# A two-layer RWKV and selective-scan stack on one core: the chains of later chunks of layer 2 planned 2.5 slots earlier, PSUM banks picked by release time, one more place in three rings, neighbouring states side by side

## The reference

```
tok = x_embed_conv.reshape(b, c, h * w).transpose(0, 2, 1)      # 3136 tokens, 192 channels
x1, x2 = layernorm(tok, g1, b1), layernorm(tok, g2, b2)
x, z   = x1 @ W_in_x.T, x2 @ W_in_z.T                           # 384 channels each
# per direction (f, and b on the reversed tokens):
xc  = silu(conv_b + causal 4-tap conv of x)
dbl = xc @ W_xproj.T                                            # 12 ranks, 16 B, 16 C
dt  = softplus(dbl[:12] @ W_dt.T + dt_bias)
h_t = exp(dt_t * A) * h_{t-1} + (dt_t * xc_t) * B_t             # 384 x 16 states
y_t = sum_n h_t * C_t + xc_t * D
out = ((y_f + y_b) * silu(z)) @ W_out.T + b_out
```

## Time and profile before

| | |
|---|---|
| median of 3 runs | 20772.64 us (20760.73 to 20794.24) |
| profiled execution | 20745.35 us, of it the span 20743.6 us |
| DVE busy | 17255.4 us, 83% |
| POOL busy | 16916.4 us, 82% |
| PE busy | 16102.5 us, 78% |
| ACT busy | 13201.7 us, 64% |

### The profile page before, as it was taken

One profiled execution on the slowest core, in us unless ns is written; L12 is line 12 of the kernel. 1 busy time (PEld: TensorE's weight loads), 2 busy tenths in 40 slices (PEclk: granted clock), 3 DMA queues, 4 the chain that ended last, 5 costly groups with the idle time before them and its releaser, 6 DMA issues. The chain is left out here.

```text
span 20743.6 us, 188446 instructions
## 1 busy us (share of the span) xinstructions
PE 16102.5 (78%) x45152; PEld 5519.4 (27%) x45152; DVE 17255.4 (83%) x13583; ACT 13201.7 (64%) x33157; POOL 16916.4 (82%) x11028
## 2 busy tenths in 40 slices
PE   7777777777777777777777777777777777777777
PEld 2222222222222222222222222222222222222222
DVE  7888978889787897878878789787887878878788
ACT  5666656666565665656656566565665656666566
POOL 6878968789687896878968789687896978969689
PEclk8888888888888888888888888888888888888888
DMA  2423424234242342423424234242342423424243
GB/s 71 106 61 100 110 61 108 63 96 109 62 108 63 98 107 62 107 63 96 109 62 107 63 97 107 62 107 64 98 106 62 110 63 100 102 62 110 63 102 101
DMA packets 1109659, 1820.18 MB, mean 88 GB/s; under 512 B 189530, under 2 KB 1053556, under 8 KB 1108404
## 3 DMA queue, kind: packets, MB, share of 16 engines
q1 hardware_dynamic: 1108404, 1806.77, 34.7%
HBM read 1083.46 MB, written 245.63 MB: 64 GB/s over the span
## 5 line engine op out<-in xcount | busy, mean ns | idle before, releaser
L1151 DVE TENSOR_TENSOR_SCAN arena<-ps,arena 128x897 f32<-128x897 f32 x5376 | 10982.2, 2065 | 2194.7 <-issue 889.4
L1354 POOL TENSOR_TENSOR arena<-arena 128x896 f32<-128x896 f32 x5376 | 9414.5, 1766 | 428.3 <-DVE arena L1151 386.1
L1285 ACT ACTIVATE ps<-arena,A 128x448 f32<-128x448 f32 x10752 | 6390.3, 627 | 3539.1 <-DVE arena L1151 3426.3
L1057 PE MATMUL ps<-arena,rep 128*64 128x448 f32 x21504 | 5831.6, 673 | 1846.0 <-POOL arena L1354 1842.3
L1346 POOL TENSOR_TENSOR arena<-arena 128x896 f32<-128x896 f32 x2688 | 4761.3, 1772 | 1494.2 <-DMA arena<-arena 1494.2
L1057 PEld LDWEIGHTS ps<-arena,rep 128*64 128x64 f32 x21504 | 1533.7, 160 | 5661.2 <-POOL arena L1354 2884.0
L1140 DVE TENSOR_TENSOR arena<-ps,arena 128x896 f32<-128x896 f32 x2688 | 2864.2, 1066 | 131.3 <-PE ps L977 114.2
L1010 PE MATMUL ps<-arena,diag 128*128 128x448 f32 x5248 | 2308.8, 586 | 270.4 <-DVE arena L1114 227.4
L1010 PEld LDWEIGHTS ps<-arena,diag 128*128 128x128 f32 x5248 | 1040.1, 205 | 1563.1 <-issue 1160.6
L1022 PE MATMUL ps<-arena,wdt 13*128 13x448 f32 x1344 | 848.2, 731 | 641.0 <-DVE arena L1120 561.5
L1049 PE MATMUL ps<-arena,skipd 128*128 128x448 f32 x1344 | 832.5, 707 | 395.2 <-DVE arena L1127 266.6
(11 more groups left out here) (171 smaller groups left out, 18843.0 us busy)
## 6 DMA issues: line engine op xcount, KB each, us to landing
arena<-bc_rows SPq DMA_DIRECT2D x3584, 224.0 KB, 4.2
arena<-arena SPq DMA_DIRECT2D x4160, 112.0 KB, 3.1
x_projected<-arena SPq DMA_DIRECT2D x112, 672.0 KB, 3.5
y_forward<-arena SPq DMA_DIRECT2D x112, 672.0 KB, 3.3
arena<-x_projected SPq DMA_DIRECT2D x112, 672.0 KB, 5.7
arena<-y_forward SPq DMA_DIRECT2D x112, 672.0 KB, 4.3
x<-in_x SPq DMA_DIRECT2D x119, 336.0 KB, 3.7
x_normed<-arena SPq DMA_DIRECT2D x112, 336.0 KB, 2.8
```

The costliest lines, as they stand in the source:

```text
L1057: m = e.matmul(ps[64 * h:64 * h + 64, YBANK, 0:T], rep[:, 0:64], pr[:, (q - 1 + h) % NPR, a * T:a * T + T], start=False, stop=p == NP - 1 ...
L1151: e.tensor_tensor_scan(rev(hh[:, q % NH, 0:W2], s), rev(decays(q)[:, 0:W2], s), rev(bb[:, q % NB, 0:W2], s), car[:, 2 * k + p % 2, n:n + 1 ...
L1285: e.activation(two(decays(q))[:, a, :], dt2[:, r % NR2, p % 2, :], ACT.Exp, scale=Am[s][:, 2 * k + p % 2, n:n + 1]).then_inc(c_ex, 1)
L1354: e.tensor_tensor(pr[:, q % NPR, :].rearrange("p (a b) -> p a b", a=2), two(hh[:, q % NH, :]), cr[:, p - p % 2:p - p % 2 + 2, :], ALU.mult ...
```

## The change

Five things are changed. The planned times of chunks i > 1 start from `PER * (i - 1) - 2.5` instead of `PER * (i - 1)`; the second convolution comes a little later forward and 2.7 slots earlier backward relative to the rest, and gates and output projections are put back by about as much as the chain is moved forward. `dd` is kept from being sent before its place in the ring of three is free. A PE job takes the bank whose last reader is planned to end first, not the other one in turn. `NB`, `NH` and `NPR` become 4, 4 and 6. The two states that lie side by side in a tile become neighbours (states 4k + 2j and 4k + 2j + 1), so that each DMA of `bl` and `cl` reads one run of 896 numbers where it read two of 448; the order of A follows.

```diff
-NB, NH, NPR = 3, 3, 4
+NB, NH, NPR = 4, 4, 6
...
-        sp.extend([(t + 3.4, "dd", i, e), (t + 5, "ud", i, e)])
+        sp.extend([(max(t + 3.4, NP * (EJ * i + e - 2) - 0.5 if i else t), "dd", i, e), (t + 5, "ud", i, e)])
...
-        t = PER * (i - 1) if i else -60
+        t = PER * (i - 1) - 2.5 * (i > 1) if i else -60
...
-            for e, (u, v) in enumerate(((4.2, 6.4), (4.3, 7.4), (6.2, 11))):
+            for e, (u, v) in enumerate(((4.2, 6.4), (4.3, 8.6 if i > 1 else 7.4), (6.2, 11))):
...
-            for e, v in enumerate((1.3, 8.7, 10.7)):
+            for e, v in enumerate((1.3, 6.0, 10.7)):
                 conv(i, e, t + v)
-            project(i, t + 15.6, (1.9, 2.3, 5), 1.5)
+            project(i, t + 15.6, (1.9, 2.3, 5.2), 1.5)
+            t += 2.5
             gate(i, 0, t + 21.6)
-            gate(i, 1, t + 24)
-            gate(i, 2, t + 31)
+            gate(i, 1, t + 26.4)
+            gate(i, 2, t + 33.4)
             for k in range(CJ):
-                o = t + 2 * PER + (4, 6)[k]
+                o = t + 2 * PER + (6.4, 7.9)[k]
...
+    last = dict(n1="nc", n2="nr", x="xe", cv="xc", xp="p1", t="td", z="z4", o="ou")
+    read = {(name, i, e): t for p in plans[1:4] for t, name, i, e in p}
+    release = {(name, i, e): read.get((last.get(name), i, e)) for _, name, i, e in plans[0]}
...
-        b = banks[k % len(banks)]
+        b = banks[k % len(banks)] if t < -10 else min(banks, key=lambda n: until.get(n, -99))
+        until[b] = release[name, i, e]
...
                     e.dma_start(br[64 * j:64 * j + 64, 2 * k:2 * k + 2, :],
-                                cd[i % 2, 4 * k + j:4 * k + 4:2, :].unsqueeze(0).to_broadcast([64, 2, T])).then_inc(s_bl[k], 16)
+                                cd[i % 2, 4 * k + 2 * j:4 * k + 2 * j + 2, :].unsqueeze(0).to_broadcast([64, 2, T])).then_inc(s_bl[k], 16)
```

More of the change, by code:

```diff
@@ L145, in side_schedule @@
     plans = [sorted(p, key=lambda a: a[0]) for p in (pe, act, dve, pool, sp)]
-    jobs, used = {}, {}
+    jobs, used, until = {}, {}, {}
+    last = dict(n1="nc", n2="nr", x="xe", cv="xc", xp="p1", t="td", z="z4", o="ou")
+    read = {(name, i, e): t for p in plans[1:4] for t, name, i, e in p}
+    release = {(name, i, e): read.get((last.get(name), i, e)) for _, name, i, e in plans[0]}
     for k, (t, name, i, e) in enumerate(a for a in plans[0] if a[1] != "dp"):
         banks = WBANK if t >= -10 else [*WBANK, 0, 1, 2, 3]
-        b = banks[k % len(banks)]
+        b = banks[k % len(banks)] if t < -10 else min(banks, key=lambda n: until.get(n, -99))
+        until[b] = release[name, i, e]
         jobs[name, i, e] = (k, b, used.get(b, 0))
@@ L1413, in layer1_sync @@
                     e.dma_start(cr[64 * j:64 * j + 64, 2 * k:2 * k + 2, :],
-                                cd[i % 2, NS + 4 * k + j:NS + 4 * k + 4:2, :].unsqueeze(0).to_broadcast(
+                                cd[i % 2, NS + 4 * k + 2 * j:NS + 4 * k + 2 * j + 2, :].unsqueeze(0).to_broadcast(
                                     [64, 2, T])).then_inc(s_cl[k], 16)
@@ L1523 @@
         arrays[f"alog{s}"] = np.ascontiguousarray(
-            v[l1 + "A_log_" + sfx].reshape(2 * EJ, 64, NP, 2).transpose(3, 1, 0, 2).reshape(128, 2 * EJ, NP))
+            v[l1 + "A_log_" + sfx].reshape(2 * EJ, 64, 4, 2, 2).transpose(3, 1, 0, 2, 4).reshape(128, 2 * EJ, NP))
         arrays[f"vece{s}"] = cols([l1 + "conv_b_" + sfx, l1 + "dt_bias_" + sfx, l1 + "D_" + sfx], 128)
```

## The result

The changed kernel takes 19415.3 us (median of 3 runs, 19388.81 to 19433.57) against 20772.64 before: ratio 0.9344, 95% interval 0.9323 to 0.9365, so 6.6% less. The forecast was 19,760 us and the measured time lies just under the low end of the range, 19,480. The profiled execution took 19415.3 us, its span is 19413.5.

What follows compares the result with a forecast made beforehand. Layer 2 was taken as held up by POOL waiting for `du2` at chunk borders. Gains of 31 + 4.3 + 5.0 + 23 = 63.3 us an image, 1013 us in all, gave 19,760 us, range 19,480 to 20,260.

Steps and rivals of the forecast that it cites:

- The chain: `td`'s end to next chunk's product takes 13.0 us; started 2.5 slots earlier, border wait falls from 5.75 to 0 to 0.4.
- E: Rival: `cl` or the landing, not `td`, binds `ud`, so `du2` arrives as before; 20,770 us within 0.2%, chance 0.04.
- D: Rival: PE stands at a bank so long that `xp` and `t` come late as before; 21,260 us, chance 0.06.
- Border, chunks 1 to 5: The border costs the scans 4.0 us a chunk; with 2.7 for side jobs less 0.5 coupling, 6.2 gained.
- Side jobs of forward chunks: Scan waits at slots 10 to 11 and 18: 1.4 and 1.3 us gained, 2.7 together, bounds 0 and 5.0.
- Chunks 6, 7 and 13: POOL's idle 4.5 and 8.5 us in chunks 6 and 7: 4.3 and 5.0 gained; chunk 13 keeps its time.
- Chunks 8 to 12: POOL's idle 5.8 us a chunk: 4.6 taken, 1.2 left for unevenly placed side jobs; 5 x 4.6 = 23.
- the next link, `ye`, is a slot and more later: 0: Both `o` get one bank, the second waiting about 4 us of PE's time; `ye` comes later, so cost 0.
- Merged rows: `bl` and `cl` landings: bounds 0 and 2.8 us off each, 0.1 by the skill-page estimate; 0 in the sum.
- C: Rival: new waits at banks and `ye` take 3 us a forward, 2 a backward chunk; 20,240 us, chance 0.22.
- B: Rival: POOL is the pace everywhere, ACT stalls nearly go, forward chunks come to 69 us; 19,490 us, chance 0.13.
- A: The main forecast, all terms as summed: 19,760 us, own range 19,560 to 19,980, chance 0.55.

Runs made afterwards that it cites:

- x6: The changed kernel with the chains 1.25 slots earlier instead of 2.5: 20318.42 us, ratio 0.9784 to the kernel before.
- x1: The changed kernel with the old rings (`NB`, `NH`, `NPR` = 3, 3, 4): 19432.49 us, ratio 0.935 to the kernel before.
- x2: The changed kernel with PE's side jobs in banks 6 and 7 in turn, as before: 19638.1 us, ratio 0.9451 to the kernel before.
- x18: The changed kernel with gates and output projections at their old times (24, 31, 4, 6): 19740.68 us, ratio 0.9499 to the kernel before.
- x3: The changed kernel with the old state order, two runs of 448 numbers a `bl` or `cl` DMA: 19432.8 us, ratio 0.9355 to the kernel before.
- x17: The changed kernel with both second convolutions at their old offsets (7.4 forward, 8.7 backward): 19935.91 us, ratio 0.9597 to the kernel before.
- x9: The changed kernel with one more product a chunk (tile 4) on DVE in forward chunks 1 to 6: 19408.47 us, ratio 0.9342 to the kernel before.
- x13: The changed kernel with the third forward convolution at 11.5 instead of 11: 19353.89 us, ratio 0.9314 to the kernel before.

## Why the forecast was too high

The chain was right, and so was the wait at the border itself. The count of 13.0 us from `td` to product against POOL's 14.0 us of work gave a wait of 0 to 0.4 us; measured 0.0 at borders 2 to 13. x6 tests the same count at half the shift and finds it within 0.7 us forward. Product waits (388.7 for 396) follow. Of the other signs, chunks 8 to 12 came as foretold (69.2 us), while the scans' waits through ACT fell not to about 5 us a chunk but to 1.4 (7.1 us in chunks 1 to 5 of image 8). `cl` did not hold SP (E falls), PE was never held long enough to delay `xp` (D falls). The rings at 0 are right (x1).

Per image the traces show 83.1 us gained (spans) where 63.3 were summed. Term by term:

- **Border, chunks 1 to 5.** 4.0 and 1.3 for slot 18, less 0.5, were taken. The two waits gave 4.0 and 1.4 in chunks 2 to 5 and nothing went to coupling; slots 17 to 23 show 4.7, since `nc` has come into them. Right, but not all that a border costs (next term).
- **Side jobs of forward chunks: the step that failed.** The forecast had 8.0 us a chunk of scan waits through ACT before it, treated two of the four places (its slots 10 to 11 and 18, the scans of slots 11 and 19) and put the others at nothing without a reason. Those ahead of the scans of slots 3 and 14 were 1.4 and 1.1 us a chunk, and both went. The first is part of what a border costs, which the forecast had put at 4.0, the scan's own wait at the border, without its echo three slots on. At slot 11 it had 1.4; 3.4 us went and 2.4 came at `xc`, 1.0. Together chunks 2 to 5 gained 10.1 us each where 6.2 were summed: 2.5 by the two waits left out, 0.5 by the coupling that did not come, the rest in smaller waits. Chunk 1, still behind its border wait, gained 5.9. This is the largest error, 3.0 us a chunk in the mean of chunks 1 to 5, 15.1 an image, 242 us in all.
- **Chunks 6, 7 and 13.** 4.3, 5.0 and 0 taken; 5.7, 7.5 and 1.3 measured (image 8 alone, from which the terms were read: 4.2, 9.9 and 1.3). They run at POOL's full load. In chunk 6 the same echo (1.4) went, in chunk 7 also most of the wait at the convolution in its middle, of which the forecast had kept a part: slot 10 goes from 5.8 to 2.5. 5.2 us an image.
- **Chunks 8 to 12.** 4.6 taken, 4.1 measured: a good size, but by luck. Slots 17 to 23 gave 4.4 and slots 0 to 5 1.9, and slots 6 to 9 took 2.0 back. The step "the next link, `ye`, is a slot and more later: 0" failed. x2 shows that the bank choice is worth 2.3 us a chunk there, 184 of its 222 us, because the sum that `ye` reads is not a slot later but behind the third convolution, which stands behind the second `o`. With the banks in turn the gain would have been 1.8. And x18 shows the moved gates, for which the sum had no term, to be worth 322 us. The forecast took a border's gain for granted and counted the edits that keep it as free.
- **Merged rows.** 0 in the sum is right, the bound of 2.8 us off a landing was far off. It came from comparing `bl` with a load of another shape. x3 against after shows 3% of packet time and 0.2 us a landing. The prediction's estimate from the Trainium skill (DMA: Bandwidth & Descriptors, Why small descriptors are slow) was 0.1 us a landing. Its 5% is the overhead within one packet of 1792 bytes; the merge halves that, which makes, as an estimate from the same figure, 2.5% of the time of the merged rows. These rows are 45% of the bytes, so it is about 1% of all packet time. The traces show about 3% of all and 0.2 us: more than the estimate, but near it beside the bound of 2.8 us. The sign that was foretold, a landing under 4.2 us, is wrong: 4.6. With the packets of before the new times have 4.8 (x3), so it is the times that made landings longer; by what, no run shows.

These terms make 15.1 + 5.2 - 2.5 = 17.8 of the 19.8 us an image that were missed. Chunk 0 lost 0.3; the other 2.3 lie between an image's last scan and the next image's first and were not followed up.

Of the rivals, C's mechanism is real but was prevented: waits at banks and at `ye` give back 222 us (x2), 322 (x18), 526 (x17), and the change comes with the edits that avoid each. B's number (19,490) is the nearest. Half of its mechanism, that the stalls through ACT nearly go and forward chunks come to 69 us, holds (68.7); the other half, POOL as the pace, holds in chunks 6, 7 and 13, not in forward chunks (x9), where A's remaining stall at slot 10 stood until x13 took it away. What decides between A, B and C is mostly one question, which I never put for all places: what makes each sum late that a `ye` reads, a side job ahead of it or a stall before it.
